# A layer of gated delta-rule attention beside an FP4 feed-forward: unit 0 ahead of P times u, the gate projection ahead of the last Q times S, and the turn of A in two halves

## The reference, cut to what matters

```python
xn = layernorm(x)                              # x: [2, 4096, 512]
# attention: gated delta rule, 16 heads, DK=16, DV=32
q, k, v = silu(causal_conv4(xn @ [qk_w, v_w].T)); g_out = xn @ g_w.T
q = l2norm(q) * DK**-0.5;  k = l2norm(k)
def step(S, (q_t, k_t, v_t, g_t, b_t)):        # over 4096 rows
    S = S * exp(g_t)
    delta = (v_t - k_t @ S) * b_t
    S = S + outer(k_t, delta)
    return S, q_t @ S
o = rms_norm(o) * silu(g_out);  attn = o @ o_w.T
# feed-forward with FP4 weights, I = 1408, scaled per group of 128 inputs
h = silu(xn @ w_gate.T) * (xn @ w_up.T);  y = h @ w_down.T
out = x + attn + y / sqrt(mean(y*y) + eps)
```

## Time and profile before

| | us |
|---|---|
| median of 3 runs | 3346.0 |
| lowest, highest | 3338.62, 3356.49 |
| the profiled execution | 3346.24 |
| its span | 3344.4 |
| PE busy, share of the span | 3162.1, 95% |
| DVE busy | 2494.0, 75% |
| POOL busy | 1918.1, 57% |
| ACT busy | 1667.5, 50% |

### The profile page before, as it was taken

One profiled execution on the slowest core, in us unless ns is written; L12 is line 12 of the kernel. 1 busy time (PEld: TensorE's weight loads), 2 busy tenths in 40 slices (PEclk: granted clock), 3 DMA queues, 4 the chain that ended last, 5 costly groups with the idle time before them and its releaser, 6 DMA issues.

```text
span 3344.4 us, 117697 instructions
## 1 busy us (share of the span) xinstructions
PE 3162.1 (95%) x45632; PEld 2269.7 (68%) x45632; DVE 2494.0 (75%) x5472; ACT 1667.5 (50%) x3306; POOL 1918.1 (57%) x2865
## 2 busy tenths in 40 slices
PE   5999999999999999999999999999999999999996
PEld 4676677766667766667766776667677667666664
DVE  6877777777777777777777777777777777777773
ACT  4544555444555544555445555445554455544452
POOL 4566555666555666555665556665556654566643
PEclk8999999999999999999999999999999999999997
DMA  3000000000000000000000000000000000000000
GB/s 117 8 21 21 5 18 21 20 21 15 12 18 21 20 21 8 15 21 21 21 21 5 18 21 20 21 14 9 21 21 20 21 5 18 21 20 21 15 3 21
DMA packets 34157, 64.93 MB, mean 19 GB/s; under 512 B 5216, under 2 KB 7008, under 8 KB 33632
## 3 DMA queue, kind: packets, MB, share of 16 engines
q1 hardware_dynamic: 29664, 52.12, 4.7%
q10 hardware_dynamic: 4096, 6.42, 0.5%
HBM read 41.75 MB, written 16.78 MB: 17 GB/s over the span
## 4 chain that ended last, share of the span: by engine, by line
PE 83%; DVE 12%; issue 4%; ACTq 1%; ACT 0%; POOL 0%; DVEq 0%; POOLq 0%
PE PS L1174 18%; PE PS L1130 13%; PE PS L1161 9%; PE PS L1162 9%; PE PS L1243 7%; PE PS L1383 7%; PE PS L1229 3%; PE PS L1308 3%; DVE arena L884 3%; DVE arena L971 2%; PE PS L1261 2%; PE PS L1279 2%; DVE arena L374 2%; PE PS L1398 2%; DVE arena L991 1%
## 5 line engine op out<-in xcount | busy, mean ns | idle before, releaser
L884 DVE SCALAR_TENSOR_TENSOR arena<-PS,sc,arena 128x256 f32<-128x256 f32 x2112 | 1006.9, 483 | 407.8 <-ACT arena L590 306.2
L1161 PE MATMUL PS<-xh,wgu 128*128 128x256 f32 x2816 | 866.1, 340 | 58.2 <-DVE arena L992 50.7
L590 ACT ACTIVATE arena<-PS,sc 128x256 f32<-128x256 f32 x704 | 333.1, 476 | 891.9 <-PE PS L1162 771.1
L1174 PE MATMUL PS<-wdn,inner 128*128 128x512 f32 x1408 | 693.2, 620 | 32.6 <-DVE inner L896 32.6
L1162 PE MATMUL PS<-xl,wgu 128*128 128x256 f32 x2816 | 700.1, 283 | 0.0
L1161 PEld LDWEIGHTS PS<-xh,wgu 128*128 128x128 f32 x2816 | 534.8, 190 | 164.5 <-issue 87.4
L492 POOL TENSOR_TENSOR arena<-arena,work 128x31 f32<-128x31 f32 (+15 forms) x992 | 554.3, 559 | 77.8
L1162 PEld LDWEIGHTS PS<-xl,wgu 128*128 128x128 f32 x2816 | 533.4, 189 | 83.2 <-issue 83.2
L488 POOL TENSOR_TENSOR work<-arena 128x31 f32<-128x31 f32 (+15 forms) x992 | 519.6, 524 | 98.8 <-POOL arena L480 11.8
L1130 PE MATMUL PS<-xnT,wqkv 128*128 128x256 f32 x2048 | 484.3, 387 | 16.8 <-ACT xnT L560 8.8
L1130 PEld LDWEIGHTS PS<-xnT,wqkv 128*128 128x128 f32 x2048 | 383.1, 192 | 84.0 <-issue 15.3
(11 more groups left out here) (150 smaller groups left out, 4626.9 us busy)
## 6 DMA issues: line engine op xcount, KB each, us to landing
xt<-in_x SPq DMA_DIRECT2D x64, 256.0 KB, 3.4
obuf<-in_x SPq DMA_DIRECT2D x64, 256.0 KB, 2.8
out<-obuf SPq DMA_DIRECT2D x64, 256.0 KB, 2.0
wqkv<-in_wqkv ACTq DMA_DIRECT2D x1, 2048.0 KB, 13.6
arena<-in_gup ACTq DMA_DIRECT2D x2, 704.0 KB, 6.4
arena<-in_dns SPq DMA_DIRECT2D x1, 1408.0 KB, 12.1
wg<-in_wg ACTq DMA_DIRECT2D x1, 1024.0 KB, 19.9
wo<-in_wo ACTq DMA_DIRECT2D x1, 1024.0 KB, 17.0
```

What stands on the lines that cost most here:

```text
L590: eng.activation(fa[:, u % 4, :], PS[:, bank(u, 0), 0:NB * P], ACT.Copy, scale=sc[:, u % 2, KB * m:KB * m + 1]).then_inc(fa_scaled.sem, 1)
L884: eng.scalar_tensor_tensor(out=fa[:, u % 4, :], in0=PS[:, bank(u, k // 2), k % 2 * NB * P:][:, 0:NB * P], scalar=sc[:, u % 2, KB * m + k:K ...
L1161: eng.matmul(o, w, xh[:, k, :], start=True, stop=False)
L1174: ins = eng.matmul(PS[:, b, :], inner[:, m, b * P:(b + 1) * P], wdn[:, m, :], start=(m == 0), stop=(m == FM - 1))
```

## The change

On PE, `gate(1, 2)` stands in front of `k_times_u(3)` and `gate(1, 3)` in front of `q_times_s(3)`, so the gate projection ends ahead of the last Q times S. Unit 0 moves from behind `p_times_u(1)` to the front of `p_times_u(0)`, unit 1 from behind `p_times_u(2)` to behind `p_times_u(1)`, and unit 2 from behind `p_times_u(3)` to behind `p_times_u(2)`; unit 3 stays last. On DVE `turn_a` leaves its place in front of `hidden(0)` and is done in two halves, each of 16 of the 32 rows of every block, behind `hidden(2)` (after unit 5) and `hidden(3)` (after unit 7). The semaphore `a_turned` counts 2 for a tile, and its two readers (the solve on POOL, `products(0)` of the next tile on DVE) wait for both. ACT, POOL and SP keep their order.

```diff
-        a_turned = signal("a_turned", 1)
+        a_turned = signal("a_turned", 2)
...
-            hold(eng, *a_turned.at(n, 1))
+            hold(eng, *a_turned.at(n, 2))
...
-                    eng.wait_ge(*a_turned.at(t, 1))
+                    eng.wait_ge(*a_turned.at(t, 2))
...
-            def turn_a():
-                if not n:
-                    return
-                eng.wait_ge(*a_done.at(n, NB))
-                eng.wait_ge(*gram_out.at(n, NB))
-                eng.transpose(la.rearrange("p j i -> p i j"),
-                              kbq[:, :, :].rearrange("p b (h i) -> p i (b h)", i=CH)).then_inc(a_turned.sem, 1)
+            def turn_a(half):
+                if half == 0:
+                    eng.wait_ge(*a_done.at(n, NB))
+                    eng.wait_ge(*gram_out.at(n, NB))
+                s = slice(half * CH // 2, (half + 1) * CH // 2)
+                eng.transpose(la[:, :, s].rearrange("p j i -> p i j"),
+                              kbq[:, :, :].rearrange("p b (h i) -> p i (b h)", i=CH)[:, s, :]).then_inc(a_turned.sem, 1)
...
             gram_products(0)
             gram_products(1)
-            turn_a()
             hidden(0)
...
                 hidden(m)
+                if m in (2, 3):
+                    turn_a(m - 2)
...
             gate(1, 1)
+            gate(1, 2)
             k_times_u(3)
-            gate(1, 2)
+            gate(1, 3)
             q_times_s(3)
-            gate(1, 3)
-
-
+
+
+            unit(0)
             p_times_u(0)
             turn_kqn(1)
             turn_q()
             p_times_u(1)
-            unit(0)
+            unit(1)
             p_times_u(2)
-            unit(1)
+            unit(2)
             p_times_u(3)
-            unit(2)
             unit(3)
```

## The result

The changed kernel takes 3413.84 us (median; 3413.21 to 3416.41), the kernel before 3345.5 beside it. The ratio is 1.0207 (95% interval 1.019 to 1.0223). The profiled execution took 3413.38 us. From the page of after: its span, the busy time of the engines, the waits that the change brought or made longer (total us, times, longest), and the shares of the chain that ended last.

The account below looks back on a forecast made before the run. The prediction took POOL's solve to bound the tile at 101.0 us. To 3346.2 us it added 68 for 31 longer tiles, 4.5 for the last tile and 26 for lost clock: 3445 us, range 3390 to 3505.

Parts of the forecast that it names:

- Something else than PE sets 101.0 us: In the kernel before, a tile's 101.0 us was claimed not to be set by PE, judging from three tiles.
- that something is the solve: POOL's solve, 38.6 us without a gap, was claimed to set the 101.0 us tile in the kernel before.
- the slack: Behind turn_t at the tile's end: the solve may be 3.45 us late before PE feels it.
- Ahead of unit 5 near 2.5 us, none ahead of down(0): PE's idle time ahead of unit 5 grows from 1.6 us to about 2.5; the 1.13 us ahead of down(0) go.
- A half turn of 1.05 us: On DVE, each half of the turn of A takes half of the whole turn's 2.1 us.
- The solve 6.3 us later: On POOL, the solve starts 6.3 us later (5.7 to 6.6), as it waits for the turn's second half.
- Nothing shortens its 31 rounds: On POOL, the solve's 31 dependent rounds keep their length, so its end is also 6.3 us later.
- PE 2.85 us late: At the projections PE waits some 2.2 and 0.7 us for ACT's copies and is 2.85 us late from there.
- The clock, +26 us: New waits at PE's projections bring 3.4 us at 1.2 GHz in half the tiles, 0.85 us a tile, 26 us.
- case C: Rival, much slower: PE falls to 1.2 GHz in each tile after the projection wait, 3471 to 3524 us; chance 0.14.
- The last tile, +4.5 us: At the program's end no projections cover the solve's delay, so the last tile's L1078 is 4.5 us late.
- The first term: The tile grows from a mean of 101.6 us to 103.8, 2.2 us for each of 31 tiles, 68 us.

Follow-up runs that it names:

- delay3: The kernel before with three more clears of the solve's matrix on POOL ahead of the solve: 3345.04 us, ratio 1.0004.
- pe_only: The kernel before with only PE's new order of gate pieces and units, the whole turn of A still ahead of hidden(0): 3403.13 us, ratio 1.0182.
- delay6: The kernel before with six more clears of the solve's matrix on POOL ahead of the solve: 3442.16 us, ratio 1.0297.
- turn_h1_pe: The kernel before with PE's new order and the whole turn of A moved behind hidden(1): 3366.91 us, ratio 1.0061.
- turn_h1: The kernel before with the whole turn of A moved behind hidden(1), PE in its old order: 3328.16 us, ratio 0.9952.
- turn_only: The kernel before with only the turn of A moved, in halves behind hidden(2) and hidden(3), PE in its old order: 3358.34 us, ratio 1.0042.
- gate_half: The kernel before with only gate(1, 2) moved ahead of the last K times u: 3364.5 us, ratio 1.0066.
- gate_only: The kernel before with only the two gate pieces moved ahead of the last K times u and Q times S: 3368.74 us, ratio 1.0062.

## Why the prediction was right, and which terms were not

The direction, the range and the mechanism of the loss held; the reading of the kernel before and several sizes did not. Step by step:

- **"Something else than PE sets 101.0 us", and "that something is the solve":** failed. It was read from three tiles. Of the 29 tiles from the third mark on in before, the 10 with no time at 1.2 GHz took 101.0 us on average, the 10 with 3.4 us of it 101.6 and the 9 with 6.8 us 102.5, so PE's clock showed in the length. POOL has 0% of the chain that ended last, and delay3 started the solve 3.4 us later for nothing. The solve was near, but not the limit. The forecast took the slack from this step, and the slack was right.
- **turn_kqn(1) 1.25 us later:** 1.39 in pe_only (40.52 against 39.13 us behind the mark). ACT's unit 0 1.2 later: 1.1. Idle time ahead of unit 1 of 0.7: 0.81. DVE's unit 2 1.9 later: 2.2. All right.
- **Ahead of unit 5 near 2.5 us, none ahead of down(0):** 2.07, and none. The second is the turn's doing alone, since pe_only keeps 1.08 there.
- **A half turn of 1.05 us:** 1.18 on average over 64. Two halves cost 0.26 us more than the whole of the earlier trace rows.
- **The solve 6.3 us later, "about 66" behind the mark:** 67.3. The step counted the tile's own delays, not that PE's wait at the projections lies behind the same mark: they end 1696.32 - 1685.96 = 10.36 us behind it, before 8.85. With these 1.5 us 65.3 + 1.5 = 66.8.
- **"Nothing shortens its 31 rounds":** failed by 0.7 us. The solve took 38.34 us on average before and 37.69 after. Why is open. In the tile shown an L488 of 128x60 near the solve's start took 0.55 us before, beside DVE's products, and 0.29 now, but on average its whole round accounts for 0.04 us; the rest is spread over many rounds.
- **PE 2.85 us late:** 103.35 - 100.98 = 2.37, 0.87 up to the mark (0.7 predicted) and 1.5 at the projections (2.15 predicted). The waits themselves, to be "2 to 3 us in every tile", are 1.0 us. The mechanism was right and this size was not.
- **The clock, +26 us:** failed, in size and sign. PE falls to 1.2 GHz near unit 5 less often than before, never for 6.8 us, and not at the projections, where the idle time comes in two pieces of 0.4 to 0.6 us. What low clock remains does not show in the periods (103.3 us on average with none, 103.4 with 3.4 us). The term had taken the wait at the projections as 2.2 us and more, and with such waits it does come: in delay6 the clock fell behind the first of these waits in 9 of the 13 tiles in which it was 2.4 us or longer, and in none of the other 16. One of these tiles, PE's row behind the wait and the window that follows:

```profile
758.33 0.91 PE L1134 MATMUL PS<-xnT,wqkv 128*128 128x256 f32 x3 [2.82 <-ACT inner L574]
...
758.00:768.00 10.00, 9.67 (x217) 7.49 (x217) 7.24 (x19) 8.41 (x19) 5.08 (x8) 0.83 0.01 2
```

So the case C, much slower by the clock, falls in after because the wait it rests on is short. The Trainium skill (TensorE: Matmul & The Clock Gate, A second HAM failure mode: psum-queue depth-cycling, the section behind the one that the prediction names) tells of a kernel whose short idle times between groups of matmuls were frequent enough for the clock to go back and forth; here only the place with the larger idle times did so, in a part of the tiles.

- **The last tile, +4.5 us:** undersized, and a term for the start was missing. PE's third mark stands at 239.33 instead of 230.46, 8.9 us later (the first solve starts 72.7 us behind its mark), and from the last mark to the end it is 3411.6 - 3236.53 = 175.1 us instead of 3344.4 - 3178.79 = 165.6.

The sum as it came out: (103.35 - 101.67) x 29 = 48.7, + 8.9 + 9.5 = 67.1 us, and 3413.38 - 3346.24 = 67.1. Predicted were 68 + 4.5 + 26. The first term used 2.2 us for 31 tiles where 1.7 for 29 was right, and the start and the end made good for it: that 68 and 67.1 agree is luck. The clock's 26 us are most of the miss between 3445 and 3414. The text put PE's order at 0.7 us a tile on PE's own path. pe_only measures 1.8, colder clock and all, and turn_h1_pe against turn_h1 1.2. In after this is hidden, as PE's own path is shorter than the loop there.

## What to carry to other kernels

Before a step on the way to a long serial stage is moved later, read that stage's slack, and not only at the engine that waits first: here `turn_t` waited 3.6 us a tile with delay3 for nothing, and 3 us more of delay cost 95 us. Two kernels with the same waits to the tenth differed by 1.6% (turn_only, after): what set the time was the length of the loop (start behind the mark + stage - lead of the next mark), so work it out instead of adding waits up, and see by the waits behind the stage, or by a run with a shorter stage, whether it is the limit. A move that closes a gap can be right in kind and wrong by one place: the same halves one `hidden` earlier turn 0.4% slower into 1.1% faster.

## What the runs showed of the hardware

- **More idle time around unit 5, more time at 1.2 GHz.** Idle time ahead of unit 5 and of down(0), and time at 1.2 GHz, mean of a tile: 1.6 and none, 0.7 us (turn_only, turn_h1); 2.1 and none, 2.1 us (after), but 1.1 in turn_h1_pe; 1.6 and 1.1, 3.3 us (before); 2.1 and 1.1, 5.2 us (pe_only). No run holds the sum and changes its split, and turn_h1_pe shows that these two idle times are not all. In single tiles of before and after it was 0, 3.4 or, in before alone, 6.8 us.
- **PE has idle times that nothing in the profile ends,** at fixed places in long runs of 32x32 matmuls, 1.0 and 0.3 us on average at the two places of gate_half, 0.7 and 0.4 at those of gate_only. Moving one or both gate pieces by one place raised them from 10 us to 42 and 34 us and the time by 0.6%.
- **A turn of half the elements costs 56% of the whole** (1184 against 2109 ns).
- **The solve's length varied for the same 62 instructions:** 37.7 us on average in after and turn_only, 38.0 to 38.5 in the others that do all of them. It does not follow how late the solve starts: in delay6 it starts latest, 69.7 us behind the mark, and takes 38.0. That it is what DVE does beside it fits the Trainium skill (GPSIMD Engine Reference, Key points), which has both engines share SBUF interfaces; no run here isolates it.
